# Sending only the routed rows of twelve tiles through the second expert layer

## The reference

```
def _mixture(inp, C, W):                 # C[n, e] is 0 except for 3 experts of row n
    y = zeros
    for e in range(12):
        y = y + C[:, e:e+1] * (inp @ W[e].T)
xf = layernorm(x)                        # 2048 rows x 256
C1, C2, C3 = the three routers' weights (softmax over each row's top 3)
h = gelu(_mixture(xf, C1, W1), approximate=False)
y = _mixture(h, C2, W2) + C3 @ b2
out = x + y
```

## Time and profile before

| | us |
|---|---|
| median of 3 runs | 409.35 (407.42 to 409.38) |
| the profiled execution's own time | 410.84 |
| its span, first to last instruction | 409.1 |
| PE busy | 393.3 (96%) |
| VectorE busy | 340.5 (83%) |
| ScalarE busy | 112.9 (28%) |
| GpSimd busy | 111.4 (27%) |

### The profile page before, as it was taken

The page is one execution under the profiler, slowest core; times in us unless marked ns, Lnnn a source line. Parts: engine busy times, 40 slices in busy tenths (PEclk is TensorE's granted clock), DMA queues, the critical chain, the costliest instruction groups (busy, mean ns, idle before and its releaser), DMA issues.

```text
span 409.1 us, 7666 instructions
## 1 busy us (share of the span) xinstructions
PE 393.3 (96%) x2132; PEld 334.5 (82%) x2132; DVE 340.5 (83%) x1038; ACT 112.9 (28%) x261; POOL 111.4 (27%) x165
## 2 busy tenths in 40 slices
PE   4889999999999999999999999999999999999996
PEld 3679889898988888888888888888888888888884
DVE  4788898998885889789898888989789898888875
ACT  2477888888932101010000100001010000100000
POOL 5264556465540211202112020211202112020200
PEclk9989999999989999999999999999999999999999
DMA  7900131322000000000000000000000000000000
GB/s 233 330 2 2 52 103 53 102 78 76 2 0 2 2 0 15 13 0 13 0 13 13 0 13 0 13 0 13 13 0 13 0 13 12 1 13 0 14 0 26
DMA packets 8613, 12.72 MB, mean 31 GB/s; under 512 B 1076, under 2 KB 5016, under 8 KB 8472
## 3 DMA queue, kind: packets, MB, share of 16 engines
q1 hardware_dynamic: 8040, 12.44, 9.2%
q10 hardware_dynamic: 560, 0.13, 0.1%
HBM read 10.47 MB, written 2.10 MB: 31 GB/s over the span
## 4 chain that ended last, share of the span: by engine, by line
PE 83%; ACT 4%; DVE 4%; issue 4%; POOL 2%; DMA 1%; ACTq 0%; POOLq 0%; DVEq 0%; SPq 0%
PE banks L936 66%; PE banks L978 2%; PE banks L1003 2%; PE banks L1013 2%; PE banks L988 2%; PE banks L991 1%; PE banks L1053 1%; PE banks L993 1%; ACT w_h L543 1%; DVE q_hl L637 1%; POOL w_l L377 1%; ACT prob L480 1%; PE banks L1061 1%; PE banks L1043 1%; DMA x_all<-in_x_dram 1%
## 5 line engine op out<-in xcount | busy, mean ns | idle before, releaser
L832 DVE SCALAR_TENSOR_TENSOR s_d<-banks,c_cur,s_d 128x256 f32<-128x256 f32 x165 | 72.7, 479 | 25.3 <-PE banks L936 22.2
L936 PE MATMUL banks<-w_h,xf_h 128*128 128x512 f32 x204 | 81.4, 399 | 0.0
L936 PE MATMUL banks<-w_l,xf_h 128*128 128x512 f32 x204 | 80.0, 392 | 0.0
L936 PE MATMUL banks<-w_h,xf_l 128*128 128x512 f32 x204 | 79.7, 391 | 0.0
L418 POOL TENSOR_TENSOR top_e<-euler,top_d 128x9 f32<-128x9 f32 x16 | 29.0, 1813 | 181.5 <-DVE top_d L782 181.5
L936 PE MATMUL banks<-w_h,h_h 128*128 128x512 f32 x180 | 73.0, 405 | 0.0
L936 PE MATMUL banks<-w_l,h_h 128*128 128x512 f32 x180 | 70.5, 391 | 0.0
L936 PE MATMUL banks<-w_h,h_l 128*128 128x512 f32 x180 | 70.1, 389 | 0.0
L832 DVE SCALAR_TENSOR_TENSOR sum<-banks,c_new,sum 128x256 f32<-128x256 f32 x160 | 66.3, 479 | 2.8 <-PE banks L936 2.7
L570 ACT ACTIVATE h_h<-banks 128x256 fp32r<-128x256 f32 x15 | 5.8, 386 | 156.4 <-PE banks L1061 156.4
L936 PEld LDWEIGHTS banks<-w_l,xf_h 128*128 128x128 f32 x204 | 38.4, 188 | 8.3
(11 more groups left out here) (129 smaller groups left out, 628.3 us busy)
## 6 DMA issues: line engine op xcount, KB each, us to landing
stage<-in_w_t_dram SPq DMA_DIRECT2D x12, 512.0 KB, 3.6
out_dram<-x_all SPq DMA_DIRECT2D x16, 128.0 KB, 1.9
x_all<-in_x_dram SPq DMA_DIRECT2D x1, 1024.0 KB, 7.8
x_all<-in_x_dram SPq DMA_DIRECT2D x1, 768.0 KB, 8.0
mask_all<-in_mask_dram SPq DMA_DIRECT2D x2, 256.0 KB, 5.2
wk_sb<-in_wk_t_dram SPq DMA_DIRECT2D x1, 256.0 KB, 3.0
x_all<-in_x_dram SPq DMA_DIRECT2D x2, 128.0 KB, 3.8
wq_sb<-in_wq_t_dram SPq DMA_DIRECT2D x1, 256.0 KB, 4.3
```

The costliest lines, as they stand in the source:

```text
L832: dve.scalar_tensor_tensor(out=sums[e % 2][:, :], in0=product, scalar=weights[:, e:e + 1], in1=sums[e % 2][:, :], op0=ALU.mult, op1=ALU.ad ...
L936: ins = pe.matmul(dst, a(c), b(c), start=(i == 0), stop=(i == len(terms) - 1))
```

## The change

Tiles 0 to 11 (S = 12) go through the second layer only for the experts that their rows are routed to; tiles 12 to 15 stay dense.

- **Layer 1 alone, tiles 1 to 12.** PE runs one slot of layer 1 a tile, with two small matmuls (`rank`) that count for every row how many rows before it picked the same expert. VectorE makes a place in a list out of it (`rows_of`). ScalarE multiplies h by each of its three weights (`weigh_h`), takes the first pair's two products off VectorE (`first_pair`), the copy of the logits and the normalisation too. GpSimd scatters the three weighted copies of a tile into `h_rows` in DRAM, with an indirect DMA each (`send_h`): a region for each expert.
- **Table.** After tile 12 VectorE works out how many blocks of 128 rows each expert has. SP fills each list's tail with zero rows, and SP and PE load the table's values into registers, 24 at a time.
- **Blocks.** 47 blocks, a number fixed in the program that holds the worst case. A block is loaded from `h_rows` (128 KB), transposed, split in high (ScalarE) and low (VectorE), multiplied by its expert's matrix with 6 matmuls of 128x256, copied out of PSUM by ScalarE and stored to `y_rows`, two blocks a store.
- **Back.** Beside the dense second layer of tiles 12 to 15, GpSimd gathers three rows for each row of tiles 0 to 11, 36 indirect DMAs (`fetch_y`), and VectorE adds each to x (`add_y`).

```diff
+    S = 12
+    FETCH_ORDER = [(g + i, k) for g in range(0, S, 2) for k in range(TOP_K) for i in range(2)]
+    REGION = (S + 1) * P
+    ZERO_ROW = EXPERTS * REGION
+    BLOCKS = (S * P * TOP_K + EXPERTS * (P - 1) + EXPERTS - TOP_K) // P
...
-        return 0 if isinstance(t, int) and t == 0 else 2 * t - 1
+        return t if t <= S else 2 * t - S - 1
     def slot2(t):
-        return 2 * T - 1 if isinstance(t, int) and t == T - 1 else 2 * t + 2
+        return T + 3 if t == T - 1 else 2 * t - S + 2
...
+    LOADS, STORES, HT, Y_BANK = 8, 4, 3, (3, 4, 6)
+    FETCHES, BATCH_REGS = 12, 24
...
+            sp.wait_ge(zeros_set, 1)
+            sp.dma_start(h_rows[ZERO_ROW:ZERO_ROW + P, :], zero_rows).then_inc(tails_set[0], 16)
+            sp.wait_ge(table, 2)
+            ends = values(mybir.EngineType.SP, end_row, ZERO_ROW)
+            for e in range(EXPERTS):
+                sp.dma_start(h_rows[bass.ds(ends[e], P), :], zero_rows).then_inc(tails_set[e * ZEROS // EXPERTS], 16)
+            first_rows = []
+            def load_block(j):
+                if j % BATCH_REGS == 0:
+                    last = min(j + BATCH_REGS, BLOCKS)
+                    first_rows.extend(values(mybir.EngineType.SP, table_rows[0:1, j:last], ZERO_ROW))
+                if j >= LOADS:
+                    sp.wait_ge(block_t, j - LOADS + 1)
+                sp.dma_start(h_in_block[j % LOADS], h_rows[bass.ds(first_rows[j], P), :]).then_inc(block_in[j % LOADS], 16)
+            sp.wait_ge(table, TABLE)
+            for i in range(2):
+                sp.wait_ge(h_sent[i], 16 * TOP_K * S // 2)
+            for i in range(ZEROS):
+                sp.wait_ge(tails_set[i], 16 * EXPERTS // ZEROS + (16 if i == 0 else 0))
+            for j in range(LOADS):
+                load_block(j)
+            for j in range(BLOCKS):
+                if j % 2 or j == BLOCKS - 1:
+                    i, n = j // 2, j % 2 + 1
+                    sp.wait_ge(block_out, j + 1)
+                    sp.dma_start(y_rows[2 * i * P:(2 * i + n) * P, :].rearrange("(b p) d -> p b d", b=n),
+                                 y_pair[i % STORES][:, 0:n * D].rearrange("p (b d) -> p b d", b=n)
+                                 ).then_inc(y_sent[i % STORES], 16)
+                if j + LOADS < BLOCKS:
+                    load_block(j + LOADS)
...
+            def send_h(t):
+                pool.wait_ge(row_set, t + 1)
+                pool.wait_ge(h_weighed, TOP_K * (t + 1))
+                for k in range(TOP_K):
+                    pool.indirect_dma_start(out=h_rows[:, :], out_offset=bass.IndirectOffsetOnAxis(h_row[:, t, k:k + 1], 0),
+                                            in_=h_w[t % 2][k], in_offset=None).then_inc(h_sent[t % 2], 16)
+            def fetch_y(i):
+                t, k = FETCH_ORDER[i]
+                if i >= FETCHES:
+                    pool.wait_ge(y_summed, i - FETCHES + 1)
+                pool.indirect_dma_start(out=y_fetched[i % FETCHES], out_offset=None, in_=y_rows[:, :],
+                                        in_offset=bass.IndirectOffsetOnAxis(y_row[:, t, k:k + 1], 0)
+                                        ).then_inc(y_back[i % FETCHES], 16)
...
+            for t in range(1, S + 1):
+                if t < S:
+                    inverse_deviation2(t + 2)
+                    exponentials(t + 1)
+                send_h(t - 1)
...
+            for i in range(8):
+                fetch_y(i)
+            split_c3(S + 1)
+            exponentials(S + 2)
...
+            def weigh_h(t):
+                act.wait_ge(h_ready, t + 1)
+                if t >= 2:
+                    act.wait_ge(h_sent[t % 2], 16 * TOP_K * (t // 2))
+                for k in range(TOP_K):
+                    nc.scalar.activation(h_w[t % 2][k], h[:, :], ACT.Copy,
+                                         scale=w_all[:, t, 1, k:k + 1]).then_inc(h_weighed, 1)
...
+            def first_pair(t):
+                act.wait_ge(route, ROUTE_STEPS * (t + 1))
+                act.wait_ge(acc, SUMS * slot1(t))
+                act.wait_ge(pair_done, PAIRS * slot1(t) + 1)
+                for e in range(2):
+                    nc.scalar.activation(sum1[e][:, :], banks[:, BANK[0], e * D:(e + 1) * D], ACT.Copy,
+                                         scale=c_all[:, t, 0, e:e + 1]).then_inc(acc, 1)
...
+            def block_high(j):
+                act.wait_ge(block_t, j + 1)
+                if j >= HT:
+                    act.wait_ge(block_done, j - HT + 1)
+                nc.scalar.activation(bt_h[j % HT], banks[:, j % HT, 0:D].rearrange("p (c t) -> p c t", c=C),
+                                     ACT.Copy).then_inc(block_hi, 1)
+            def block_copy(j):
+                act.wait_ge(block_done, j + 1)
+                i = j // 2
+                if i >= STORES:
+                    act.wait_ge(y_sent[i % STORES], 16 * (i // STORES))
+                nc.scalar.activation(quarter(y_pair[i % STORES], j % 2), banks[:, Y_BANK[j % HT], 0:D], ACT.Copy).then_inc(block_out, 1)
...
+            def add_y(first, last):
+                for i in range(first, last):
+                    t, k = FETCH_ORDER[i]
+                    if k > 0:
+                        dve.wait_ge(y_summed, FETCH_ORDER.index((t, k - 1)) + 1)
+                    dve.wait_ge(y_back[i % FETCHES], 16 * (i // FETCHES) + 16)
+                    dve.tensor_tensor(x_all[:, t, :], x_all[:, t, :], y_fetched[i % FETCHES], ALU.add).then_inc(y_summed, 1)
...
+            experts(S, (0, 0, 2))
+            experts(S + 1, (2, 9, 12))
+            experts(S + 2, (12, 20, 27), ahead=False)
             start_layer2(T - 1)
-            layer2_pairs(T - 1, range(PAIRS))
+            layer2_pairs(T - 1, range(4))
+            add_y(27, S * TOP_K)
...
+            def rank(t):
+                pe.wait_ge(z_copied, t + 2)
+                pe.wait_ge(sel_set, t + 1)
+                if t > 0:
+                    pe.wait_ge(taken_set, t)
+                else:
+                    pe.wait_ge(rank_consts, 10)
+                pe.matmul(ps_rank, before[:, :], picked[:, :], start=True, stop=False)
+                pe.matmul(ps_rank, ones_b[:, :], taken[:, :], start=False, stop=True).then_inc(rank_done, 1)
...
+            for t in range(1, S + 1):
+                pe.wait_ge(xf_lo, t + 1)
+                expert_pairs(slot1(t), range(0, 2), xf_parts(t), 0)
+                transpose_xf(t + 1)
+                expert_pairs(slot1(t), range(2, 4), xf_parts(t), 0)
+                if t == S:
+                    transpose_table()
+                else:
+                    logits(t + 1)
+                expert_pairs(slot1(t), range(4, PAIRS), xf_parts(t), 0)
+                if t == S - 1:
+                    row_ends()
+                if t < S:
+                    rank(t)
+                else:
+                    logits(S + 1)
...
+            def transpose_block(j):
+                pe.wait_ge(block_in[j % LOADS], 16 * (j // LOADS) + 16)
+                if j < HT:
+                    pe.wait_ge(acc, SUMS * S + 2 * j + 2)
+                else:
+                    pe.wait_ge(block_lo, j - HT + 1)
+                for c in range(C):
+                    ins = pe.transpose(banks[:, j % HT, c * P:(c + 1) * P], h_in_block[j % LOADS][:, c * P:(c + 1) * P],
+                                       ident[:, :])
+                ins.then_inc(block_t, 1)
+            def multiply_block(j):
+                start = first_weights[j]
+                pe.wait_ge(block_lo, j + 1)
+                if j < HT:
+                    pe.wait_ge(acc, SUMS * S + 2 * (j + HT) + 2)
+                else:
+                    pe.wait_ge(block_out, j - HT + 1)
+                part = lambda w: lambda c: w[:, bass.ds(start + c * 2 * D, D)]
+                split_product(banks[:, Y_BANK[j % HT], 0:D], (lambda c: bt_h[j % HT][:, c, :], lambda c: bt_l[j % HT][:, c, :]),
+                              (part(w2_h), part(w2_l))).then_inc(block_done, 1)
...
+            load_weight_places(0)
+            transpose_block(0)
+            transpose_block(1)
+            for j in range(BLOCKS):
+                if j == BATCH_REGS - 4:
+                    load_weight_places(BATCH_REGS)
+                if j + 2 < BLOCKS:
+                    transpose_block(j + 2)
+                multiply_block(j)
+                if j % 3 == 2 and 1 <= j // 3 <= S:
+                    expert_bias(j // 3 - 1)
+                if j % 3 == 1 and 1 <= j // 3 <= S:
+                    transpose_c3(j // 3 - 1)
+            pe.wait_ge(block_lo, BLOCKS)
```

More of the change, by code:

```diff
@@ L311, in _, with values @@
                              w_dram[layer][:, :, pair * 2 * D:(pair + 1) * 2 * D]).then_inc(w_in[n % RING], 16)
[L313 to L320 removed]
+            def values(engine, row, most):
+                return nc.values_load_multi_w_load_instructions(
+                    row, engines=[engine], min_val=0, max_val=most,
```

(1 more changed line is left out.)

486 lines of the change are left out of this document (376 added, 110 removed).

## The result

The changed kernel takes 380.55 us (median of four, 379.05 to 380.99) against 408.38 for the kernel before in the same comparison (407.22 to 409.38): ratio 0.9313, 95% interval 0.9271 to 0.9355. Its profiled execution took 379.05 us with a span of 377.3. The prediction was 379, in a range of 363 to 405. The total came out closer than its terms, as the rest of this text shows.

What follows compares the result with a forecast made beforehand. PE's matmul count was taken to pace the expert stage. Start 135.7, loop 102.3, table 18.3, blocks 55.0 and tail 66.9 gave a 378.2 us span, 378.4 in time, rounded up to 379; range 363 to 405.

Steps and rivals of the forecast that it cites:

- Start and loop: Layer 1 of tile 1 starting at 135.7, then the layer-1 loop over tiles 1 to 11, 102.3 us.
- Three loads of 8.5 to 9.1 interlock, so I take 9.3: Layer-1 loop: PE 9.1, VectorE 8.8 and a ScalarE-VectorE cycle of some 8.5 us together give 9.3 a tile.
- The ring: Layer-1 loop: ScalarE-VectorE dependency cycle, some 8.5 us; as rival, each handover 0.2 more, 10.3 a tile, 390; chance 0.09.
- Tile 12 and the table: From tile 12's slot to the first block product: VectorE's table, loads, PE's wait, lower clock; 18.3 us, bounds 15 and 24.
- Blocks: 47 blocks of routed rows at 1.17 us each: 55.0 us, bounds 47 and 64.
- Tail: Seven dense slots, last sums and last store behind the blocks: 64.4 + 2.5 us, bounds 64.4 and 75.
- must fit in the tail: 36c + 6 for the other POOL work is 49 at c = 1.2: Tail: 36 gathers at c, POOL's time per indirect DMA, plus 6 us of other POOL work take 49 us.
- The port: VectorE reading two SBUF operands shares a port with GpSimd reading SBUF, the second waiting; the trace neither confirmed nor denied it.
- Gathers late in part: Tail: each gather held by up to one 0.42 us addition, 14 us more, half hidden; 387; chance 0.15.
- POOL becomes the bound: Loop and tail: indirect DMAs at 2.39 us of POOL each, +9 and +27, 415; chance 0.12.
- Blocks at half clock: Blocks: short pieces don't hold PE's clock, matmuls at 0.21, a block at 1.9, +34, 413; chance 0.06.
- PE-paced in all three stages: Whole forecast as summed: PE sets the pace throughout, 366 to 394; chance 0.52.

Runs made afterwards that it cites:

- the kernel with spare products: Changed kernel plus 24 unread 128x512 products on PE while the first block's rows are on their way; 382.45 us, ratio 0.9373.
- fixed places: Changed kernel with block weights at constant places, so no place loads or address instructions on PE and rows don't meet their own expert's weights; 377.80 us, one execution.
- the additions alone: Changed kernel without gathers on POOL; VectorE's 36 additions stay and add what the buffers hold; 376.83 us, one execution.
- two other edits: Changed kernel with zero-row stores split over two queues, SyncE's places loaded early, and 9 spare products on PE; 376.61 us, ratio 0.9214.

## Why the prediction came out as it did

*Start and loop.* 133.7 for 135.7 and 101.1 for 102.3. The step "Three loads of 8.5 to 9.1 interlock, so I take 9.3" was wrong by 0.2 a tile: PE alone sets 9.08, even with VectorE at 95%. (The ring's pieces as I listed them add up to 8.7 before any handover, not to 8.5 with them; either way it didn't bind.) Only the first tile, where ScalarE's copies come late, took 10.3. The start was off by less than it varies between executions.

*Tile 12 and the table.* 19.7 for 18.3, inside its bounds, by another mechanism. I had VectorE's table as the string and left out of SyncE's work the twelve stores of zero rows: 12 issues of 0.47 and a landing of 1.9 would have been 7.5 us. I had the table at 11 us from the slot's start and the first block's rows 3.5 behind it. The table stood at 9.7 (244.51), the stores had landed at 248.42, and the rows 8.2 behind the table (252.75). The idle stretch was 7.5 us, not 3 to 5. That the total is near is luck: the table 1.3 early, and 2 us that I added here for the lower clock. That clock cost 1.2 to 1.6 us, by the kernel with spare products, and most of it lies in the blocks.

*Blocks.* 51.6 for 55.0. The term took 1.17 with address instructions "nearer the upper end because ScalarE has little slack". They cost nothing (fixed places), ScalarE is not in the way, and a block is 0.93, or 1.07 where bias work stands between, which was 0.14 a block and not 0.08; my lower bound was 1.00. What no term held is PE's second load of places, 1.8 us of idle time.

*Tail.* 71.2 for 66.9. "PE's 60.7 us stays" and "the end slips by 1.5 to 2" are right: 55.83 twice, and 2.5 for the additions alone. The step that failed is that the gathers "must fit in the tail: 36c + 6 for the other POOL work is 49 at c = 1.2", and so cost nothing. The sum was right in c (1.25) and wrong in what it left out: POOL works in order, its exponentials and bias splits for the last tiles stand behind gathers, and a gather behind VectorE's additions. That was 4.35 us. With the additions spread and POOL's order as it was, the tail was 58.46 again, so what stood behind the gathers came late for the held gathers more than for its place.

*The port.* The kernel before had no row for it, and I left it out of the sum. Here the rows have it: the eight kernels whose additions, both inputs in SBUF, stood in strings beside gathers have 22 gathers of 1.7 to 3.2 us, of which 20 ended 0.81 to 0.83 us after a string (two 0.4 to 0.5 after it); the three with the additions spread have none over 1.3. The Trainium skill, SBUF — State Buffer, Who interferes with whom, says that a VectorE instruction with two SBUF inputs contends with a GpSimd one that reads SBUF: by that rule, the trace agrees. The same section of the Trainium skill infers that such an instruction does not hold up the making of descriptors; here a gather, which makes them, was held up. Whether it was held at reading its 128 places from SBUF or at writing descriptors, no run separates; as a gather takes 0.95 alone and ended 0.82 behind the string, all but some 0.13 us of its own work came behind it, by this estimate. Nor did POOL get in between two additions of 0.34 us when it had been caught, as a lock for a single instruction would allow; other gathers did pass through a string at 1.0 to 1.2 us, and which ones are caught isn't known.

*The rivals.* "Gathers late in part" had it at 387 with every gather held by one addition; what happened is few gathers held by whole strings, 4 us instead of 7. "POOL becomes the bound" did not happen at 1.25, but once PE was earlier VectorE's last addition waited 3.04 us for the last gather. "Blocks at half clock" was true of the first blocks alone, 1.2 to 1.6 us of its 34. The ring left no trace beyond the first tile.

So that the total was right to 1 us is luck: terms of both signs met, blocks -3.4, start and loop -3.2, against tail +4.3 and table +1.4. The last step had luck too: I took 1.5 us off because the median before lay that much below its profiled execution; after the change it lies 1.5 above (380.55 to 379.05). Its mechanism, PE-paced in all three stages, holds for the loop and the blocks, and not for the two seams.

## What to carry to other kernels

Where a POOL queue makes the descriptors of gathers, don't let VectorE run additions of two SBUF operands in a string beside it: the same additions two at a time shortened the tail by 4.2 us, and by 3.8 on top of two other edits, where the medians show 2.4. Behind a long in-order queue of DMAs the engine's own small pieces become someone's wait, so look what stands behind them, and count small stores on the issuing queue when a table is built (the twelve stores landed 3.9 us behind the table). When a gain is read from medians of two chips, look whether a stretch that neither edit touches took the same time in both. When terms are checked by distances inside one execution, a total that agrees no longer hides two that don't.

## What the runs showed of the hardware

- An indirect DMA of 128 rows of 1 KB takes 0.95 us of POOL, with 0.30 to the next, both as scatter (0.96 to 0.97) and as gather. In the traces that record landings, a gather lands 2.8 or 2.9 us after its start and a scatter 2.4 to 2.6, by the medians.
- Loading 24 or 23 values into registers took PE's queue 2.37 and 2.81 us in the changed kernel (2.1 to 3.0 in the others) and SyncE 1.43 and 1.84 (up to 2.8). PE works off what its queue held before and is then idle, 1.79 us at the second load.
- Products whose weights stand at an address from a register ran as fast as at a fixed one (0.12 each), four address instructions among six.
- The same twelve issues on SyncE took 8.9 to 9.0 or 6.2 us in different executions, and all profiles of one chip showed the same of the two. Of what differs between the chips the record has no more than that.
- Behind 7.5 and 3.9 us without work PE ran its first 4.3 and 3.6 us at the lower clock level (products 0.21 apart), and 3.3 and 6.4 us behind the waits of 6.27 and 5.46; behind 1.8 us at the second load of places it did not (0.12).
- The count by which PE reports its products came late in some executions, by PE's own records: 9.5 us at the longest (357.71 to 367.24). The seven profiles of the second and third chip show none of it.
